# A recurrent transformer kernel on one core: two orders on TensorE's queue, slots 0 and 1 of each step

## What is computed

```python
for i in range(DEPTH):                                   # 6 layers
    x = attn_layer(shift_tokens(x), Wqkv[i], ...) + x    # 16 heads of 64, windows of 32 tokens looking one window back
    x = ffn_layer(shift_tokens(x), ...) + x              # LayerNorm, 128 -> 2 x 341, exact gelu gate, 341 -> 128
```

## Time and profile before

| | us |
|---|---|
| median of 3 runs | 1732.7 |
| lowest and highest run | 1731.18, 1740.07 |
| span of the profiled execution (its own time beyond the span is not listed) | 1731.0 |
| TensorE busy | 1639.0 (95%) |
| VectorE, ScalarE, GpSimd busy | 1446.3, 1425.6, 1311.9 |
| mean granted TensorE clock | 0.986 of full speed |

### The profile page before, as it was taken

One profiled execution on the slowest core, in us unless ns is written; L12 is line 12 of the kernel. 1 busy time (PEld: TensorE's weight loads), 2 busy tenths in 40 slices (PEclk: granted clock), 3 DMA queues, 4 the chain that ended last, 5 costly groups with the idle time before them and its releaser, 6 DMA issues.

```text
span 1731.0 us, 68758 instructions
## 1 busy us (share of the span) xinstructions
PE 1639.0 (95%) x25970; PEld 1277.2 (74%) x25970; DVE 1446.3 (84%) x3011; ACT 1425.6 (82%) x2851; POOL 1311.9 (76%) x1305
## 2 busy tenths in 40 slices
PE   7779999999999999999999999999999999999995
PEld 5657777777777777777777777777777777777773
DVE  4499888888888888888888888888888888888884
ACT  3367888888888888888888888888888888888885
POOL 6088877877877787787778778787877877777765
PEclk9799999999999999999999999999999999999997
DMA  4111111111111111111111111111111101111000
GB/s 140 41 38 43 35 33 36 30 48 38 41 32 30 36 36 42 49 30 32 30 36 42 49 36 30 32 30 48 38 41 36 30 27 38 35 30 32 28 24 26
DMA packets 41426, 66.40 MB, mean 38 GB/s; under 512 B 7072, under 2 KB 16032, under 8 KB 41376
## 3 DMA queue, kind: packets, MB, share of 16 engines
q1 hardware_dynamic: 40224, 65.38, 12.7%
q10 hardware_dynamic: 1152, 0.34, 0.1%
HBM read 20.61 MB, written 1.05 MB: 13 GB/s over the span
## 4 chain that ended last, share of the span: by engine, by line
PE 61%; ACT 28%; issue 6%; DVE 4%; ACTq 1%; DMA 0%; POOL 0%; DVEq 0%; POOLq 0%
PE ps_qs L530 12%; PE ps_po L530 9%; PE ps_q L530 8%; PE ps_a L530 7%; PE ps_tk L530 7%; PE ps_f L530 6%; PE ps_po L650 5%; ACT p_bd L943 4%; PE ps_k L530 4%; PE ps_v L530 4%; ACT squares L949 4%; ACT L1053 3%; ACT L1050 3%; ACT q_t L943 3%; ACT prob L987 2%
## 5 line engine op out<-in xcount | busy, mean ns | idle before, releaser
L427 POOL TENSOR_TENSOR qk<-qk,rnorm 128x512 f32<-128x512 f32 x384 | 393.6, 1046 | 176.6 <-DVE rnorm L1284 176.1
L419 POOL TENSOR_TENSOR qk<-qk,qk_rot 128x512 f32<-128x512 f32 x384 | 483.8, 1282 | 0.0
L434 POOL TENSOR_TENSOR prob<-prob,row_inv 128x512 f32<-128x512 f32 x192 | 200.7, 1045 | 92.8 <-DVE row_inv L1301 92.8
L1289 DVE TENSOR_REDUCE row_max<-ps_qs 128x8 f32<-128x512 f32 x191 | 132.0, 691 | 164.8 <-PE ps_qs L530 164.8
L943 ACT COPY p_bd<-ps_po 64x512 f32<-64x512 f32 x378 | 219.1, 580 | 58.8 <-PE ps_po L650 56.4
L1264 DVE TENSOR_REDUCE ssq<-squares 128x8 f32<-128x512 f32 x384 | 261.4, 681 | 3.4 <-ACT squares L949 3.4
L530 PEld LDWEIGHTS ps_qs<-k_t,q_t 64*32 64x32 f32 x12224 | 179.2, 107 | 69.0 <-issue 68.9
L943 ACT COPY attn_t<-ps_po 128x512 f32<-128x512 f32 x191 | 112.5, 589 | 133.2 <-PE ps_po L530 133.1
L530 PE MATMUL ps_qs<-k_t,q_t 64*32 64x64 f32 x12224 | 210.1, 218 | 0.0
L530 PE MATMUL ps_po<-p_bd,v_back 128*64 128x64 f32 x3056 | 193.2, 225 | 0.0
L530 PEld LDWEIGHTS ps_po<-p_bd,v_back 128*64 128x64 f32 x3056 | 163.1, 137 | 35.8 <-issue 17.0
(11 more groups left out here) (237 smaller groups left out, 4082.7 us busy)
## 6 DMA issues: line engine op xcount, KB each, us to landing
v_back<-v_own SPq DMA_DIRECT2D x192, 192.0 KB, 2.4
w_raw<-in_wqkv SPq DMA_DIRECT2D x48, 192.0 KB, 2.4
v_back<-v_own SPq DMA_DIRECT2D x96, 64.0 KB, 2.1
wo_sb<-in_wo SPq DMA_DIRECT2D x12, 256.0 KB, 2.9
w_sb<-in_w SPq DMA_DIRECT2D x6, 341.0 KB, 3.1
w_sb<-in_w SPq DMA_DIRECT2D x6, 192.0 KB, 2.7
x_in<-in_x SPq DMA_DIRECT2D x4, 256.0 KB, 4.2
out<-s_out SPq DMA_DIRECT2D x8, 128.0 KB, 1.9
```

The costliest lines, as they stand in the source:

```text
L419: nc.gpsimd.tensor_tensor(qk[:, s, i, :], qk[:, s, i, :], qk_rot[:, s, i, :], ALU.add).then_inc(added, 1)
L427: nc.gpsimd.tensor_tensor(heads(qk[:, s, i, :]), heads(qk[:, s, i, :]), rnorm[:, s, 8 * i:8 * i + 8].unsqueeze(2).to_broadcast([P, 8, HEAD ...
L434: nc.gpsimd.tensor_tensor(heads(prob[:, s, :]), heads(prob[:, s, :]), row_inv[:, s, :].unsqueeze(2).to_broadcast([P, 8, HEAD]), ALU.mult). ...
L1289: V.tensor_reduce(row_max[:, s, :], heads(ps[:]), AX, ALU.max).then_inc(max_done, 1)
```

## The change

In TensorE's `body`, two pieces of the queue change places; nothing is added or removed, and the other engines' code is as before. In slot 0 `ln_spread(n-3)` is issued in front of `out_projection(n-2, 1)` instead of behind it. In slot 1 `ff_down(n-4)` is issued behind `values` instead of in front of it.

```diff
                     if j == 0:
+                        if live_batch(n - 3):
+                            ln_spread(n - 3, u)
                         if live_batch(n - 2):
                             out_projection(n - 2, 1)
-                        if live_batch(n - 3):
-                            ln_spread(n - 3, u)
                     if j == 1:
                         if live_batch(n - 2):
                             ln_mean(n - 2)
                         if live_batch(n - 3):
                             ff_up(n - 3, 0)
-                        if live_batch(n - 4):
-                            ff_down(u - 2, n - 4)
...
                     if live(u - 4):
                         values(u - 4, n - 1, j, j % 2)
+                    if j == 1 and live_batch(n - 4):
+                        ff_down(u - 2, n - 4)
```

## The result

The changed kernel took 1691.18 us (median of 4 runs, 1690.09 to 1694.27) against 1732.34 before (4 runs). The ratio is 0.9752, with a 95% interval from 0.9724 to 0.9781. The forecast was 1691. The span of the profiled execution is 1689.5 us, the run's own time 1691.3; before, the span was 1731.0.

A forecast was written before the change was run, and what follows sets the result against it. The prediction took ScalarE's path from turn_p to the k copy, on which TensorE's ff_down waits, to bound the step. 44 steps x 0.94 us = 41.4, so 1732.7 - 41.4 = 1691.3 us, range 1684 to 1701.

The forecast's parts named there:

- What bounds it: Slots 0 and 1: ScalarE's path from turn_p to the k copy, 12.83 us against TensorE's 11.96, makes ff_down wait 0.87.
- Part 1: Slot 1, values in front of ff_down: the step loses 2.39 - 1.45 = 0.94 us if ScalarE's path stays longer.
- Part 2: Slot 0, spread in front of the half projection: two changes of matmul shape fewer, 0.34 us less of TensorE's time.
- the 0.16: At ff_down: TensorE alone would arrive 0.16 us behind ScalarE's signal without the spread's move, which had to cover that.
- my first rival: At ff_down: TensorE's path rules, the spread's move gives 0; 0.87 or 0.78 us a step, 1694 to 1698; chance 0.22.
- The wait left over: At ff_down in slot 1: TensorE still waits about 0.2 us (0.1 to 0.3) for the k copy, 44 times.
- Who comes late next: Slot 2, starting 0.94 us earlier: VectorE's row maximum has 0.48 to spare, GpSimd 0.2 at rnorm; nobody is late.
- The sum: Whole step: falls by 0.94 to 32.70 us, 44 x 0.94 = 41.4 us in all, span 1689.6.

The follow-up runs named there:

- E6: Kernel before, with ScalarE copying the turned k ahead of the turned q in slot 1; 1711.8 us, ratio 0.988.
- E2: Kernel before, with only the spread moved in front of slot 0's half projection; 1734.1 us, ratio 1.001.
- E4: Changed kernel with the spread back behind the half projection and ScalarE's k copy ahead of its q copy in slot 1; 1692.5 us, ratio 0.9776.
- E7: Changed kernel with, in slot 1, ScalarE's k copy ahead of its q copy and VectorE's sum of q's squares ahead of newton; 1675.3 us, ratio 0.9652.
- E1: Changed kernel with the spread back behind the half projection, so only values ahead of ff_down remains; 1691.9 us, ratio 0.9764.
- E3: Changed kernel with ScalarE's k copy ahead of its q copy in slot 1; 1682.4 us, ratio 0.9722.
- E8: The changed kernel repeated with nothing else altered, timed against the kernel before; 1694.7 us, ratio 0.977.

## Why the prediction was right, point by point

**What bounds it.** Right. E6 (a shorter path of ScalarE in the old kernel) and E2 (a shorter one of TensorE) tell it: the first pays in full, the second nothing.

**Part 1.** Right. Forecast: 0.94 us a step, made of 2.39 less 1.45. Measured: from `ff_down`'s start to the q projection 895.74 - 894.28 = 1.46, the step shorter by 0.94. The 0.09 for a full-width matmul behind it was read from another group, the output projection, and held. What was reckoned to follow it did: ScalarE's wait in slot 2 went.

**Part 2.** Forecast: 0.34 us of slot 0, swallowed but for 0.16. Slot 0 from k transposes to q projection is 886.90 - 883.11 = 3.79 for 4.14; E2's wait grew by 0.34, E4 against E7 gives 0.34. How it was swallowed was also as said: E1 without it is within 0.02 us a step. Only the 0.16 was mis-sized. I counted the FFN product to its modelled end, 1.02 us, where the next group starts after 892.98 - 892.03 = 0.95, and gave `values` 1.03, where E3 has 0.98 to `ff_down` (887.56 to 888.54). That is 0.12 of it. The rest is `ff_down` itself, which takes 1.41 to the q projection where TensorE doesn't wait in front of it (E4, 895.33 to 896.74), for the 1.45 that I reckoned. E4, which has TensorE's queue as E1 and no wait, has TensorE's path at 32.71 against ScalarE's 32.70: there was about nothing to cover, and part 2 is worth about nothing in this change. It also means that the time alone couldn't have told my forecast from my first rival, for which I had 1694 to 1698: with the slot 0 of before, TensorE's path sets the same step and about the same time (E1 1691.9, E4 1692.5). That the forecast was right about which path rules is shown by E2, E3 and E7, not by the 1691. That two changes of shape fewer make slot 0 shorter is shown for this pair of orders; that it is the drain which the Trainium skill ("TensorEngine Tiling (Array Packing)", Key Properties) speaks of agrees with it, but the runs don't separate a drain from a weight load that can't be hidden behind the neighbour.

**The wait left over.** Forecast: about 0.2 us (0.1 to 0.3), 44 times, in the list of waits, and a chain still through ScalarE. The cause was right, the size too small, and the sign by which to see it wrong. From the first matmul of `values` to `ff_down` TensorE takes 894.28 - 892.98 = 1.30 in the changed kernel, and 0.98 in E4, where the k copy is early and nothing is waited for:

```profile
894.35 0.34 PE L530 MATMUL ps_po<-p_bd,v_back 128*64 128x64 f32 x4
...
895.33 1.48 PE L530 MATMUL ps_tk<-ff_m,w_sb 128*64 128x257 f32 x12
896.74 0.50 PE L530 MATMUL ps_q<-w_hi,xs_hi 128*128 x1
```

So the wait is 0.32 us, and `ff_down` takes 1.46 behind it for 1.41 without it. Slot 1 is 8.84 us long in the changed kernel and 8.47 in E4 and E7, and the step is 0.34 longer than E7's. The wait is larger than I said because there was nothing for part 2 to cover. The list doesn't show it, and the chain shows a gap of 0.15, because the modelled end of `values` hides the rest: where TensorE doesn't wait, it reaches 0.18 past the start of `ff_down` (E3, 888.43 + 0.29 against 888.54). The chain goes over TensorE at 92%, where the kernel before had 61%. Read alone, that would have said that TensorE rules.

**Who comes late next.** In the changed kernel nobody, as forecast. The row maximum of slot 2 had 0.49 us to spare for the 0.48 forecast:

```profile
897.79 0.69 DVE L1289 TENSOR_REDUCE row_max<-ps_qs 128x8 f32<-128x512 f32 x1 [0.49 <-PE ps_qs L530]
898.51 0.69 DVE L1292 TENSOR_TENSOR prob<-ps_qs,row_max 128x512 f32<-128x512 f32 x1
899.12 0.47 DVE L1278 SCALAR_TENSOR_TENSOR rn_a<-ssq_c,rn 128x18 f32<-128x18 f32 x1
```

GpSimd's spare time was 0.54 us where I had 0.2, because `newton` takes 0.3 longer: its first operation is 0.47 for 0.17. ScalarE's start values aren't the reason, since they are ready at 897.69; the operation starts at 899.12 while GpSimd's `w_lo` is running and ends 0.03 behind it (899.59 and 898.55 + 1.01 = 899.56). Before, `w_lo` was over at 919.57 and `newton` began at 920.04. I looked at slots 2 and 3 one wait at a time and so missed both that VectorE was near to having no hole from slot 1 on and that an earlier `newton` would run into GpSimd's work; that is why E3's expectation, and not this change's, failed.

**The sum.** 44 x 0.94 = 41.4; the spans differ by 41.5. The step, 32.70 forecast and measured, is what this confirms. That the medians agree with the forecast to some tenths is luck, since the runs of one kernel lie 4 us apart and the same kernel took 1694.7 in E8.

## What to carry to other kernels

Where an engine waits for another inside a periodic pipeline, find the point from which both paths start and write down both lengths: a change pays up to the difference of the two and no further, whatever the busy share says. Put work whose inputs are long ready in front of the instruction that waits, and then look for the next path within a few tenths of a microsecond; here ScalarE's, then VectorE's, then TensorE's own lay at 32.70, 32.50 and 32.36 us. A chain of waits that runs over the busiest engine is no proof that it rules where modelled ends overlap by as much as the gap that is left: compare starts with those of a kernel that doesn't wait there. Lengthen the other engine by a known amount and see if the step grows by all of it, then shorten it to see by how much it rules. And where an engine comes earlier, look at what its neighbours are doing at that time: one operation of VectorE grew from 0.17 to 0.83 us because it now started beside one of GpSimd's.

## What the runs showed of the hardware

The order of matmul groups on TensorE has a price of its own. The same four spread matmuls, the same 16 projection matmuls and the same 32 of `values` take 0.34 us less when the two 64-column groups stand side by side. It showed in E2's waits and in E4 against E7, at the full clock in both.

A small operation of VectorE (`newton`'s first, 128x18 in float32) that starts while GpSimd runs `w_lo` or the second `ff_m` ends only 0.02 to 0.04 us behind GpSimd's operation: it takes 0.37, 0.47 or 0.83 us for 0.17, by how long GpSimd still has to run. It showed in the kernel before (slot 1), in the changed kernel (slots 1 and 2) and in E3; what in the chip holds it back no run here separates.
